# Gated cross-attention block on one core: one product for the diagonals of two heads, a projection ahead of the values, one division per pair

## What is computed

```python
x = x + tanh(g_xattn[0]) * mlstm(layernorm(x), ctx, ctx)        # 4 heads
x = x + tanh(g_ffn[0]) * switch_head_attention(layernorm(x))    # 8 heads, 5 experts
x = x + tanh(g_xattn[1]) * perceiver(ctx, mask, layernorm(x))   # 16 heads of 64
x = x + tanh(g_ffn[1]) * moe(layernorm(x))                      # 8 experts, the best one
```

```python
x, lat = _layernorm(features, gm, bm), _layernorm(latents, gl, bl)
q = lat @ Wq                                  # 256 rows, 16 heads of 64
k, v = concat([x, lat]) @ Wk, concat([x, lat]) @ Wv   # 512 rows
sim = einsum('bhqd,bhfd->bhqf', q * SCALE, k)
sim = sim - max(sim, axis=-1)
sim = where(kv_mask, sim, -inf)
out = einsum('bhqf,bhfd->bhqd', softmax(sim), v) @ Wo
```

## Time and profile before

| | us |
|---|---|
| median of 3 runs | 827.13 (826.36 to 827.43) |
| the profiled execution | 821.55 |
| its span, first to last instruction | 819.8 |
| busy in the span: TensorE, VectorE, GpSimd, ScalarE | 623.1, 644.3, 414.4, 328.5 |
| first to last `take_max` | 403.4 to 693.6 |
| mean granted TensorE clock, of full speed | 0.881 |

### The profile page before, as it was taken

One profiled execution on the slowest core, in us unless ns is written; L12 is line 12 of the kernel. 1 busy time (PEld: TensorE's weight loads), 2 busy tenths in 40 slices (PEclk: granted clock), 3 DMA queues, 4 the chain that ended last, 5 costly groups with the idle time before them and its releaser, 6 DMA issues.

```text
span 819.8 us, 16271 instructions
## 1 busy us (share of the span) xinstructions
PE 623.1 (76%) x5721; PEld 377.6 (46%) x5721; DVE 644.3 (79%) x1199; ACT 328.5 (40%) x565; POOL 414.4 (51%) x353
## 2 busy tenths in 40 slices
PE   6499667895595586561687889788878887789997
PEld 5376422542342343340334445444544455657776
DVE  5757898499689789879487888698779777478886
ACT  2333100421321321320265666466556664356651
POOL 4432366066356446885554545355444455256662
PEclk9999968598699599575599999999999999889999
DMA  7211000000000000040000000000000000000000
GB/s 195 65 32 53 27 0 0 1 1 2 1 0 0 0 0 0 22 132 27 26 1 2 2 2 1 4 2 2 2 3 2 2 1 2 2 1 0 0 0 26
DMA packets 14168, 13.04 MB, mean 16 GB/s; under 512 B 3120, under 2 KB 11936, under 8 KB 14112
## 3 DMA queue, kind: packets, MB, share of 16 engines
q1 hardware_dynamic: 14112, 12.25, 5.2%
HBM read 11.72 MB, written 0.52 MB: 15 GB/s over the span
## 4 chain that ended last, share of the span: by engine, by line
PE 43%; DVE 39%; issue 10%; ACT 3%; POOL 2%; DVEq 1%; DMA 1%; ACTq 0%; SPq 0%; POOLq 0%; PEld 0%
DVE nmax L1255 8%; DVE work L722 5%; DVE work L780 5%; DVE diag L1262 3%; PE banks L1733 3%; PE banks L1040 2%; PE banks L1063 2%; PE banks L470 2%; PE banks L1071 2%; PE banks L1439 2%; PE banks L1065 2%; PE banks L1064 2%; PE banks L1440 2%; PE banks L1441 2%; PE banks L1045 2%
## 5 line engine op out<-in xcount | busy, mean ns | idle before, releaser
L1378 POOL TENSOR_TENSOR attn<-work,attn 128x512 f16<-128x512 f32 (+1 forms) x96 | 142.1, 1482 | 147.4 <-ACT attn L1165 147.4
L722 DVE TENSOR_TENSOR work<-banks,gatev 128x512 f32<-128x512 f32 x120 | 79.0, 682 | 14.2 <-PE banks L472 13.8
L1255 DVE TENSOR_REDUCE nmax<-banks 128x2 f32<-128x1024 f32 x64 | 77.7, 1215 | 15.3 <-PE banks L1025 14.8
L1063 PE MATMUL banks<-work,attn 128*128 128x65 f16 x512 | 54.4, 200 | 44.9 <-DVE nmax L1255 37.9
L1262 DVE TENSOR_SCALAR diag<-identb,nmax 128x128 bf16<-128x128 bf16 x128 | 81.5, 677 | 2.2
L1063 PEld LDWEIGHTS banks<-work,attn 128*128 128x128 f16 x512 | 48.8, 101 | 59.6 <-DVE nmax L1255 42.5
L1486 POOL TENSOR_SCALAR work<-work 128x512 f16<-128x512 f32 x64 | 53.0, 851 | 35.8 <-ACT work L1418 33.1
L470 PE MATMUL banks<-weights,xbTh 128*128 128x512 f16 x120 | 49.6, 414 | 28.0 <-DVE work L722 26.1
L1424 DVE TENSOR_TENSOR work<-work 128x512 f16<-128x512 f32 x64 | 57.0, 949 | 12.2 <-POOL work L1486 12.2
L850 POOL TENSOR_TENSOR work<-work 128x512 f32<-128x512 f32 x24 | 30.4, 1267 | 62.0 <-DVE work L722 59.7
L1733 PE MATMUL banks<-ident,work 128*128 128x128 f32 x276 | 53.0, 330 | 8.6 <-DVE work L1933 3.0
(11 more groups left out here) (280 smaller groups left out, 1970.9 us busy)
## 6 DMA issues: line engine op xcount, KB each, us to landing
stage<-in_L_ffn_w SPq DMA_DIRECT2D x8, 512.0 KB, 3.8
stage<-in_L_ffn_Wkv SPq DMA_DIRECT2D x4, 640.0 KB, 3.9
stage<-in_L_ffn_Wq SPq DMA_DIRECT2D x2, 640.0 KB, 4.7
xt<-in_x SPq DMA_DIRECT2D x1, 512.0 KB, 4.2
ct<-in_ctx SPq DMA_DIRECT2D x1, 512.0 KB, 5.5
wo<-in_L_xattn_Wo SPq DMA_DIRECT2D x1, 512.0 KB
stage<-in_L_xattn_Wv SPq DMA_DIRECT2D x1, 512.0 KB, 3.4
stage<-in_L_xattn_Wq SPq DMA_DIRECT2D x1, 512.0 KB, 3.4
```

The lines of the kernel that those rows point to most:

```text
L722: dve.tensor_tensor(heads8(m.prod[:, k, e, :]), heads8(bank_pj[c % 2][:, :]), wide(g, DH1), ALU.mult).then_inc(s.prod_ready, 1)
L1063: pe.matmul(o, ph, vh, start=(kt == 0), stop=False)
L1255: dve.tensor_reduce(m.nmax[:, p % 2, i, :], banks[:, 6:8, :], AX.X, ALU.max, negate=True).then_inc(s.c_max_done, 1)
L1378: pool.tensor_tensor(m.Pl[:, p % 2, kts, :], m.Pf[:, kts, :], m.Ph[:, p % 2, kts, :], ALU.subtract).then_inc(s.c_P_lo, 1)
```

## The change

TensorE issues job "h" directly behind job "f", ahead of the values. VectorE issues the `low` of job "f" ahead of `take_out`, and that of "h" stays behind it. `spread_max` becomes one instruction with two tensor operands: the identity (bfloat16), repeated for two heads, times the two columns of negated maxima (float32), each repeated 128 times. `take_out` divides both heads by one product of 256 elements where there were two of 128.

```diff
@@ pe_c, step
                 if t + 1 < STEPS_C:
                     row_max(it, t + 1, 1)
-                if "f" in jobs:
-                    job(it, (t, "f"), jobs["f"])
+                for place in "fh":
+                    if place in jobs:
+                        job(it, (t, place), jobs[place])
                 if t >= 1:
                     values(it, t - 1, t)
                 if b >= 1 and n in (2, 4):
                     project_ao(it, n // 2 - 1, job_no[t - 1, "c"], bank_wo)
-                if "h" in jobs:
-                    job(it, (t, "h"), jobs["h"])
@@ dve_c, spread_max
-                for h in range(2):
-                    at = (h * I + i) * P
-                    ins = dve.tensor_scalar(m.diag[:, p % 2, at:at + P], m.identb[:, :], m.nmax[:, p % 2, i, h:h + 1], None, ALU.mult)
-                ins.then_inc(s.c_D_ready, 1)
+                dst = m.diag[:, p % 2, :].rearrange("p (h i c) -> p h i c", h=2, i=I)[:, :, i, :]
+                dve.tensor_tensor(dst, m.identb[:, :].unsqueeze(1).to_broadcast([P, 2, P]), wide(m.nmax[:, p % 2, i, :], P), ALU.mult)\
+                    .then_inc(s.c_D_ready, 1)
@@ dve_c, take_out
-                for hh in range(2):
-                    ins = dve.tensor_tensor(dst[:, hh, :, :], O[:, hh, :, 0:DH2], wide(den[:, 2 * hh:2 * hh + 2], DH2), ALU.mult)
-                return ins
+                return dve.tensor_tensor(dst, O[:, :, :, 0:DH2], den.rearrange("p (h i) -> p h i", h=2).unsqueeze(3).to_broadcast([P, 2, I, DH2]), ALU.mult)
@@ dve_c, step
                     spread_max(it, t + 1, 1)
+                if "f" in jobs:
+                    low(it, (t, "f"), jobs["f"])
                 if t >= 1:
                     ins = take_out(it, t - 1)
                     if b >= 1 and n in (2, 4):
                         ins = add_x3(it, b - 1, n // 2 - 1, bank_wo)
                     ins.then_inc(s.c_O_free, 1)
-                for place in "fh":
-                    if place in jobs:
-                        low(it, (t, place), jobs[place])
+                if "h" in jobs:
+                    low(it, (t, "h"), jobs["h"])
```

## The result

| | before | after |
|---|---|---|
| median, us | 826.83 (4 runs, 826.36 to 827.43) | 789.89 (4 runs, 786.93 to 794.82) |
| ratio | | 0.956 (0.950 to 0.962) |
| the profiled execution; its span | 821.55; 819.8 | 794.82; 793.1 |
| span up to the first maximum | 403.4 | 403.8 |
| first to last maximum (called the stage here) | 290.2 | 258.5 |

The kernel is 36.9 us faster by the medians and 26.7 by the two profiled executions. The profiled run of the change is the slowest of its four; the four spans go from 785.2 us (mean granted clock 0.89) to 793.1 (0.881).

What follows compares the result with a forecast made beforehand. Neither engine is full: TensorE and VectorE wait for each other in turn. 10.1 + 1.4 + 1.9 + 13.0 + 1.5 + 2.6 - 0.15 - 0.7 gave 29.7 us off, 827.13 to 797.5; range 788 to 818.

Steps and rivals of the forecast that it cites:

- the clock's 2.6: Drops of the granted clock to 0.50 behind TensorE's idle, 1.7 us each; half of three counted as gained, 2.6 us.
- Single product, uncontended: VectorE's one product, not held by GpSimd, takes 0.42 us like the old pair: no difference; bounds 0.24 and 0.67.
- Single product, held: VectorE's product ends 0.27 us behind GpSimd; no second instruction to hold (second block): 10.1 + 1.4 + 1.9 us.
- Job "h" ahead of the values: Even steps: TensorE's values start 4.42 us after R, the step's first `row_max`; next R at 7.20, 1.00 shorter.
- In steps 1 to 3 I count 1.5 together: Gain from moving job "h" in the first steps, where VectorE also has the latents' norms: 1.5 us together.
- Steps 4, 6, ... 28, 13.0 us: Even steps become bound by TensorE with job "h" ahead of the values, each 1.00 us shorter: 13.0 us.
- The order of remainder and division does not matter: VectorE, odd steps: the next row maxima wait for both, in either order; next R at 8.25 against 8.20.
- The thinnest cover: Even steps: VectorE's keys' remainder ends at R+6.05, the values at about 6.1; covered by 0.05 to 0.25 us.
- Rival C: ScalarE's copy, later than R+6.0, delays remainder and reciprocal: 0.68 us in all 28 steps with job "h", 833.5; chance 7%.
- The first subtraction is nearly over when the products come: Even steps: GpSimd's first subtraction nearly ends before VectorE's products at R+1.80, so the values can start at 4.42.
- The division: VectorE's one division takes 0.42 us for 0.49; hidden in even steps, within the 8.25 of odd ones.
- Rival A: GpSimd does not hold VectorE's new product; odd steps 7.2 instead of 8.25, 13.6 us more, 784; chance 10%.

Runs made afterwards that it cites:

- e6: The changed kernel with all three GpSimd subtractions cut to 8 of 512 columns, leaving out most remainders; 773.8 us, ratio 0.939 to 0.943.
- e8: The kernel before with all three GpSimd subtractions cut to 8 of 512 columns, leaving out most remainders; 793.4 us, ratio 0.961 to 0.971.
- e2_product: The kernel before with the single product alone; 808.3 us, ratio 0.969 to 0.986.
- e1: The kernel before with the two moves alone (job "h" ahead of the values, keys' remainder ahead of `take_out`); 802.4 us, ratio 0.962 to 0.984.
- e7_unrolled: The changed kernel with TensorE's loop of three turns written out, the other engines keeping theirs; 790.3 us, ratio 0.958 to 0.966.
- e4: The changed kernel with the keys' remainder (`low` of job "f") back behind `take_out` on VectorE; 792.5 us, ratio 0.950 to 0.966.
- e5: The changed kernel with GpSimd's widest subtraction (1024 elements) written as two of 512; 787.1 us, ratio 0.951 to 0.962.
- e9: The changed kernel with the negated maxima written into PSUM instead of SBUF; 780.3 us, ratio 0.931 to 0.945.
- e3: The kernel before with one division per pair alone; 825.3 us, ratio 0.996 to 1.003.

## Why the prediction was right, and where it was not

The forecast was 797.5 with 788 to 818; 789.9 came, 7.6 us under the forecast and near the low end. In the profiled execution it gave 791.9 and 794.8 came. The sum of 29.7 us came near the stage's 31.8 partly by luck, since its terms were off both ways. Steps 1 to 3 gave 6.8 us for 3.6 forecast and the odd steps from 5 on 15.1 for 9.8 (the clock's 2.6 among them), while the even steps from 4 on gave 9.8 for 14.4 and step 30 nothing in the stage for 1.9. The mechanism of both kinds of step was right: even steps went to TensorE, odd ones stayed with VectorE behind GpSimd.

- **Single product, uncontended: right.** Taken as 0.42 for 0.42; 0.42 to 0.43 came where nothing held it, and e6 and e8 have 27.3 and 26.7 us for all. The two rows that the prediction took for products of two tensors, L704 and L1424, are subtractions with the same two kinds of operand; their times held for the product. The estimate by the Trainium skill's VectorE: DVE Perf Modes, table of modes, of 0.2 us more per pair is not borne out at this size: the two forms cost the same. The prediction set the second start of the pair against the longer stream; how much each is no run shows.
- **Single product, held: right.** It is held, and ends at 486.84 (484.57 + 2.27), 0.28 behind GpSimd (484.44 + 2.12 = 486.56), for 0.27 forecast (672 - 426 is 0.25; the slip is 0.02 us a step). The second blocks are gone: none of the 64 lasts over 2281 ns, where the last pair of the earlier trace rows took 3.21 us. Its terms were 10.1 + 1.4 + 1.9, and with the clock's 2.6 made 16.0; e2_product had 17.0. But the 1.9 was step 30's, whose product comes behind the last maximum and so outside of the stage, which leaves 14.1 for the 17.0. There the pair of 3.21 us became a product of 1.36, and yet the last step's first subtraction, the matmuls that wait for it, starts 4.52 us behind the last maximum before, 3.68 in e2_product and 5.50 in the change, whose clock is 0.50 from there on for some 7 us. So that term is 0.8 where it is seen and not 1.9.
- **Job "h" ahead of the values: right for even steps.** 7.20 forecast, 7.19 measured, with TensorE never waiting in front of step 8's values. They start 0.10 ahead of the forecast (+4.32 for +4.42), and what follows takes 2.88 for 2.78. For odd steps 8.25 was forecast and 8.13 measured. The bound is the one named, GpSimd's hold.
- **"In steps 1 to 3 I count 1.5 together": too small.** These steps went from 11.04, 10.72 and 9.16 to 7.49, 8.22 and 8.37, 6.8 us in all. With the 2.1 of the second blocks I had 3.6 there. e1 alone takes 2.7 of it and e2 3.3.
- **"Steps 4, 6, ... 28, 13.0 us": two of them did not go.** Steps 12 and 20 hold the turn of the loop and took 12.53 and 11.91 for 11.96 and 11.55. I priced all even steps by step 8, though the trace of before named TensorE's idle there, 1.91 us. It is 2.43 now, and the 1.0 of each was not had. e7_unrolled shows that the branch holds them there, by its idle and the clock behind it. Together they lost 0.9 us where 2.0 were counted as gained, most of what the even steps came short.
- **"The order of remainder and division does not matter": wrong as a statement, harmless in the sum.** e4 changes odd steps by 0.58 and even ones by 0.43 the other way. The order moves the start of the odd step's product across GpSimd's. I had looked at how long things take and not at who starts first.
- **The thinnest cover was gone in step 8, at no cost.** The remainder starts at R+5.40, as forecast, and ends at +6.09; the values end at +5.96 for about 6.1 forecast, and the reciprocal starts at +6.01 with no idle in front of it. So VectorE's remainder ends last by a few hundredths, and even steps do not feel it, because TensorE reaches the next R at +7.20 only. Rival C needed ScalarE's copy later than R+6.0 in all steps: it was so in steps 3 (+7.25) and 21 (+6.04) alone.
- **"The first subtraction is nearly over when the products come": right, but by the odd step's own lateness.** e5 shortens odd steps, and the even step's product is held again. So an odd step cannot be mended alone; e9 mends both.
- **The division: hidden, as forecast.** e3 has 0.999 (0.996 to 1.003). That a step can win or lose 0.9 by which engine goes first was not foreseen; whether the division did that in e3 stays open.
- **The clock: mis-sized.** The stage before had six drops of 3.4 us to 0.50 (at 423.4, 433.6, 515.5, 590.6, 648.7 and 686.2 us), and I had counted three. Each cost more than the 0.87 that I took: with a second block step 11 takes 10.66 with a drop and steps 5 and 13 take 9.20 without one, and step 13 of e3_division takes 10.77 with one, so some 1.5 us. That is some 2 us of the 5.3 that the odd steps gave over the forecast, and it helped e2_product too, which has one drop left. Steps 13 and 21, behind the turns of the loop, gave 3.1 where 1.9 was counted. None of the six is left. The stage after has two new ones, at 515.9 and 584.2 us, both just behind a turn of the loop, where TensorE had stood 2.43 and 2.05 us. But the execution profiled has drops behind the stage too. Two stretches of it, columns as the earlier trace rows, and the whole part behind the stage:

```profile
700.30:703.70 3.40, 3.40 (x34) 3.40 (x34) 3.40 (x7) 0.00 (x0) 1.57 (x2) 0.50 0.00 0
782.20:789.00 6.80, 6.80 (x56) 6.38 (x56) 2.37 (x8) 0.00 (x0) 0.00 (x0) 0.50 0.15 41
662.27:793.10 130.83, 114.79 (x1224) 86.13 (x1224) 91.41 (x198) 58.68 (x87) 63.08 (x73) 0.91 0.02 5
```

The part behind the stage took 126.2 us at a clock of 0.93 before. By these 4.6 us, and 0.4 ahead of the stage, 31.8 us of the stage come out as 26.7 in the profiled execution. In all twelve profiles this part takes 123.1 to 130.9 and the part ahead of the stage 403.4 to 412.6, in code that the edits touch only at the end of the attention, in the first 15 us or so of the later part. No run here forces the clock, so that the clock makes these differences is argued from its rows and not shown. The medians' 36.9 is over the 31.8 of the stage, and how much of the rest is such scatter stays open.

**Rival A**, that GpSimd does not hold the new product, was false of the change. It is what e9 then made true: its price was 13.6 us more, and e9's stage is 14.9 shorter than that of the change. In time 784 was forecast for it, and 780.3 (770.9 to 781.0) came.

## What to carry to other kernels

When an instruction of VectorE takes several times what the same line takes elsewhere, and its end lies just behind that of a GpSimd instruction, count its inputs in SBUF before shortening anything: moving two floats per row to PSUM was worth 14.9 us of the stage, more than the reordering of GpSimd's work or of VectorE's queue. Where two engines alternate like this, mend both halves of the loop at once, since a step that is early moves the collision into its neighbour; and price each step by its own timeline, for those with a loop's branch or another job in them do not follow the pattern. Judge a change of this size by the stretch that it touches as well as by the whole, because the parts around it moved by 8 and 9 us between profiles.

## What the runs showed of the hardware that I had not expected

- Joining two products into one costs or saves nothing by its own length (26.7 and 27.3 us for all), but one instruction is held once where a pair could be held twice; with the drops of the clock that went with it, that gave 17.0 us of the stage.
- Whichever goes first pays nothing and the other all of it: 0.04 us ahead, the product took 0.43 and GpSimd's subtraction 0.25 more; 0.13 behind, the product took 2.27. Within 0.03 us the recorded starts do not say which went first.
- A branch leaves TensorE idle for 2.43 us, more than a third of a step of 7.2, where it was 1.91 before the change, and the clock fell right behind it.
